# Input layernorm by batch, and a reordered opening, in a two-axis Mamba block with experts

## The reference, cut to what matters

```python
x = x + conv(ln(x, eps=1e-6))         # ln over the 64 channels, no weight
t = tokens(x)
t = t + experts(ln(t, eps=1e-5))      # 16 experts, the best 2 of each token
...
def dual_path(x, ...):                # conv above
    for i in range(6):
        xt = xt + mamba2(rmsnorm(xt, t_norm[i]), ...)   # sequences along time, per band
        xb = xb + mamba2(rmsnorm(xb, b_norm[i]), ...)   # sequences along bands, per time
def mamba2(x, ...):
    z, xBC, dt = split(x @ Win)
    x, B, C = split(silu(causal_conv4(xBC)))
    dt = softplus(dt + dt_bias)
    h[t] = exp(-dt * exp(A_log)) * h[t-1] + dt * x[t] * B[t];  y[t] = h[t] . C[t] + D * x[t]
    return rmsnorm(y * silu(z), gnorm) @ Wout
```

## Time and profile before

| | |
|---|---|
| three timed runs | 1254.06, 1256.41, 1258.2 us; median 1256.41 |
| the profiled execution | 1250.45 us, span 1248.5 us |
| TensorE | busy 1094.0 us, 88% of the span |
| VectorE | 836.2 us, 67% |
| ScalarE | 756.2 us, 61% |
| POOL | 312.1 us, 25% |
| mean granted TensorE clock | 0.966 of full speed |

### The profile page before, as it was taken

One profiled execution on the slowest core, in us unless ns is written; L12 is line 12 of the kernel. 1 busy time (PEld: TensorE's weight loads), 2 busy tenths in 40 slices (PEclk: granted clock), 3 DMA queues, 4 the chain that ended last, 5 costly groups with the idle time before them and its releaser, 6 DMA issues.

```text
span 1248.5 us, 46550 instructions
## 1 busy us (share of the span) xinstructions
PE 1094.0 (88%) x20216; PEld 568.9 (46%) x20216; DVE 836.2 (67%) x1219; ACT 756.2 (61%) x1450; POOL 312.1 (25%) x306
## 2 busy tenths in 40 slices
PE   2699989999999999989989999998987339999998
PEld 1355555555555545555454555555544223333332
DVE  4378666787666876668766687666876565656564
ACT  2477777677777677767777767776765113333332
POOL 7422232332223223232232322323222400000000
PEclk9799999999999999999999999999999558999999
DMA  4100110201111011110111101111000500000000
GB/s 84 23 18 7 30 30 19 44 5 31 31 31 33 2 31 31 31 32 4 30 31 31 33 2 31 31 31 33 9 7 14 85 1 1 1 9 9 1 9 9
DMA packets 66354, 28.75 MB, mean 23 GB/s; under 512 B 53416, under 2 KB 61928, under 8 KB 66152
## 3 DMA queue, kind: packets, MB, share of 16 engines
q1 hardware_dynamic: 66152, 25.78, 9.7%
HBM read 9.96 MB, written 1.05 MB: 9 GB/s over the span
## 4 chain that ended last, share of the span: by engine, by line
PE 72%; DVE 11%; issue 8%; ACT 6%; POOL 1%; DMA 1%; SPq 0%; ACTq 0%; DVEq 0%; POOLq 0%
PE ring L681 14%; PE ybank L766 10%; PE ring L893 6%; DVE em L1275 5%; PE ybank L908 5%; PE ring L746 5%; PE ring L899 4%; PE oss L778 4%; PE ring L705 4%; PE ring L691 4%; PE oss L781 3%; PE ring L633 2%; PE xtb L735 2%; PE ring L723 2%; ACT rstd L971 1%
## 5 line engine op out<-in xcount | busy, mean ns | idle before, releaser
L1275 DVE TENSOR_TENSOR em<-em,gs 128x1536 f32<-128x1536 f32 (+1 forms) x192 | 296.4, 1565 | 8.4 <-ACT em L1004 7.8
L1004 ACT ACTIVATE em<-ring 128x512 f32<-128x512 f32 x480 | 248.4, 597 | 9.5 <-PE ring L746 5.5
L766 PE MATMUL ybank<-em,xdt 64*32 64x64 f32 (+1 forms) x12288 | 186.7, 238 | 26.3 <-issue 19.5
L566 POOL TENSOR_TENSOR ysq<-yg 128x512 f32<-128x512 f32 x96 | 130.6, 1360 | 282.9 <-DVE yg L1295 282.9
L766 PEld LDWEIGHTS ybank<-em,xdt 64*32 64x32 f32 x12288 | 154.1, 106 | 83.9 <-issue 55.2
L746 PE MATMUL ring<-rt,lt 128*64 128x512 bf16 x960 | 144.9, 393 | 9.7 <-ACT em L1004 6.1
L1148 ACT ACTIVATE em<-ring 128x512 f32<-128x512 f32 x128 | 69.5, 595 | 137.4 <-PE ring L893 137.4
L1303 DVE TENSOR_TENSOR on<-oss,rr 128x256 f32<-128x256 f32 x96 | 40.6, 423 | 150.5 <-ACT rr L1014 150.5
L1446 DVE TENSOR_TENSOR em<-em,ring 128x512 f32<-128x512 f32 x128 | 82.2, 684 | 83.6 <-PE ring L899 81.3
L1012 ACT ACTIVATE rr<-oss,eps 128x256 f32<-128x256 f32 x96 | 45.5, 474 | 112.1 <-PE oss L781 111.9
L1282 DVE SCALAR_TENSOR_TENSOR yt<-xs,col,ybank 128x256 f32<-128x256 f32 x192 | 83.1, 473 | 35.5 <-PE ybank L766 35.3
(11 more groups left out here) (166 smaller groups left out, 1514.0 us busy)
## 6 DMA issues: line engine op xcount, KB each, us to landing
x_b<-x_t SPq DMA_DIRECT2D x48, 128.0 KB, 3.0
cm<-bc SPq DMA_DIRECT2D x24, 224.0 KB, 2.7
rt<-lt SPq DMA_DIRECT2D x120, 24.0 KB
cw<-in_L_conv_t_cw SPq DMA_DIRECT2D x6, 320.0 KB, 3.3
cw<-in_L_conv_b_cw SPq DMA_DIRECT2D x6, 320.0 KB, 3.1
x_in<-in_x SPq DMA_DIRECT2D x4, 256.0 KB, 4.4
xs<-in_L_ffn_w SPq DMA_DIRECT2D x2, 512.0 KB, 7.0
zs<-in_L_ffn_w SPq DMA_DIRECT2D x2, 512.0 KB, 9.1
```

The lines of the kernel that those rows point to most:

```text
L566: pool.tensor_tensor(out=ysq[c % 2][:], in0=yg[c % 2][:], in1=yg[c % 2][:], op=ALU.mult).then_inc(s_ysq, 1)
L766: mm = pe.matmul(ybank[QUAD * q:QUAD * (q + 1), ab, to:to + hi - lo], xdt[m % 2][rows, 8 * (i % 2) + 4 * first + q, r, :], em[rows, p % EM ...
L1004: emptied(act.activation(em[:, p % EM_SLOTS, :, HALF * j:HALF * (j + 1)], o.rearrange("p (h t) -> p h t", h=HEADS), ACT.Exp), "seg", n, i, ...
L1275: dve.tensor_tensor(e, e, gs[n % 2][:, i:i + 1, 0:wide].to_broadcast([P, HEADS, wide]), ALU.mult).then_inc(s_w, 1)
```

## The change

The first layernorm is made batch by batch: batch 0 first, batch 1 later, among VectorE's and ScalarE's other work of the opening. x of batch 1 is loaded behind the weights of pass 0, with a semaphore of its own. On TensorE B and C are projected ahead of x, the second batch's features and the parts are turned between the two projections of x, and mean(1, 0) comes behind z. C rows are sent before the wait for the template copies. On POOL the template's first nine selects, `tok1h` and the time parts come before the weights of pass 0; constants of the band pass and of the gate come behind `xdt`, with a fifth count `n_const[4]` that VectorE awaits in block 1. The second layernorm runs the same helpers half by half. The diff, cut:

```diff
     t.one("mean", 0, 1)
-    t.one("mean", 1, 0)
     t.two("dt", 0)
     t.one("dt_turned", 0)
+    t.two("bc", 0)
     t.one("cum", 0)
     t.two("x", 0, 0)
-    t.two("bc", 0)
+    t.one("parts", 0)
     t.two("x", 0, 1)
-    t.one("parts", 0)
     t.two("z", 0, 0)
     t.two("z", 0, 1)
+    t.one("mean", 1, 0)
     t.four("gram", 0)
...
# SP
+            x_load(0)
             weights_in(0)
+            x_load(1)
             weights_in(1)
             cross(0)
+            c_rows(0)
             sp.wait_ge(s_rep, 12)
-            c_rows(0)
             target_rows(0)
...
# POOL: h_b and tri[1] leave the front
-            const(pool.memset(h_b[:], 0.0))
...
+            parts_ones(0)
+            const(pool.memset(tok1h[:], 0.0))
+            select(tok1h[R_TOK:P].rearrange("p (a t) -> p a t", a=2), [[0, 2], [-1, HALF]], 0, 1, ALU.not_equal, 1.0)
+            n_const[1] = made[0]
+
+            const(pool.memset(rtmpl[:], 0.0))
+            for r in range(NPART):
+                select(rtmpl[0:R_TGT, LL], [[-1, HEADS], [0, HALF]], -HEADS * r, 1, ALU.not_equal, -1.0)
+                select(rtmpl[0:R_TGT, LH], [[-1, HEADS], [0, HALF]], -HEADS * r, 1, ALU.not_equal, -1.0)
+                select(rtmpl[R_HIGH:R_HIGH + R_TGT, HH], [[-1, HEADS], [0, HALF]], -HEADS * r, 1, ALU.not_equal, -1.0)
...
             weights_made(0)
+            pool.wait_ge(s_wp, 1)
             for blk in (LL, HH):
                 select(rtmpl[R_TOK:P, blk], [[0, HEADS], [1, HALF]], 0, -1, ALU.is_ge, FAR)
...
             for u in range(2):
                 const(pool.memset(xdt[u][:], 0.0))
+            n_const[3] = made[0]
+            const(pool.memset(h_b[:], 0.0))
+            const(pool.memset(tri[1][:], -1.0))
...
+            parts_ones(1)
...
             weights_made(1)
...
# PE
             mean(0, 1)
-            mean(1, 0)
             project_dt(0)
             turn_dt(0)
+            project_bc(0)
             sum_dt(0)
             project_x(0, 0)
-            project_bc(0)
+            pe.wait_ge(s_ln1, 2 * LN_STEPS)
+            to_features(s_tp, lambda j: sq[:, P * j:P * j + P], 1, 6)
+            turn_parts(0)
             project_x(0, 1)
-            pe.wait_ge(s_const, n_const[1])
-            turn_parts(0)
             project_z(0, 0)
             project_z(0, 1)
+            mean(1, 0)
             gram(0)
+            pe.wait_ge(s_x0, NCK)
             turn_x(0, 0)
...
# ACT
             rstd_of(0, 1)
-            square_x(1, 0)
+            norm_scalar(1, eps6)
+            copy_dt(0)
             exp_a(0)
-            exp_a(1)
-            rstd_of(1, 0)
-            copy_dt(0)
             softplus(0)
             act.preload_act_table_set("silu_and_others")
+            silu_bc(0)
             silu_x(0, 0)
-            silu_bc(0)
+            square_x(1, 0)
             silu_x(0, 1)
             silu_z(0, 0)
             silu_z(0, 1)
             act.preload_act_table_set("natural_log_exp_and_others")
+            rstd_of(1, 0)
+            exp_a(1)
             copy_gram(0)
...
# DVE (center: sum, scale, subtract; each over 1024 of the 2048 columns)
+            dve.wait_ge(s_ld[0], 16 * 2)
+            center(0)
+            sum_squares(0)
+            divide(0)
+            from_banks(0, 4, x_t)
...
             h_of(0, 1)
-            bias_dt(0)
-            finish_dt(0)
+            dve.wait_ge(s_ld[1], 16 * 2)
+            center(1)
             dve.wait_ge(s_const, n_const[1])
-            split_cum(0)
-            dve.wait_ge(s_const, n_const[2])
             for u in range(2):
                 dve.memset(lt[0:HALF, u], 0.0).then_inc(s_rep, 1)
...
+            sum_squares(1)
+            bias_dt(0)
+            divide(1)
+            finish_dt(0)
+            split_cum(0)
+            dve.wait_ge(s_const, n_const[2])
             for i in range(NPAIR):
                 dve.tensor_copy(rt[:, :, :, i, :].rearrange("p b h t -> p (b h) t"),
...
+            dve.wait_ge(s_rep, 4)
+            rows_of_cum(0)
+            from_banks(1, 6, x_t)
             dve.wait_ge(s_const, n_const[3])
             x_dt(0, 0)
...
# DVE, second layernorm
-            norm_vector(1)
-            from_banks(1, x2)
+            for k in (2, 3):
+                center(k)
+                sum_squares(k)
+                divide(k)
+            for k in (2, 3):
+                from_banks(k, 2 * (k % 2), x2)
```

More of the change, by code:

```diff
@@ L211, in build @@
         stat2 = sb("stat2", [P, NJ * 2])
-        s_ld = sem("x_loaded")
+        s_ld = [sem(f"x{b}_loaded") for b in range(NBATCH)]
         s_const = sem("constants_made")
@@ L358, in _, with x_load @@
         def _(sp):
-            for b in range(NBATCH):
+            def x_load(b):
                 for half in range(2):
-                    sp.dma_start(x_in[:, 8 * b:8 * (b + 1), half, :], token_rows(a["x"], b, half, 0, 8)).then_inc(s_ld, 16)
+                    sp.dma_start(x_in[:, 8 * b:8 * (b + 1), half, :], token_rows(a["x"], b, half, 0, 8)).then_inc(s_ld[b], 16)
             def weights_in(g):
@@ L496, in _, with parts_ones @@
             n_const[0] = made[0]
+            def parts_ones(s):
+                const(pool.memset(parts[s][:], 0.0))
+                for ab in range(2):
+                    rows = slice(HALF * ab, HALF * (ab + 1))
+                    const(pool.memset(parts[s][rows, :, R_TGT + NPART * ab:R_TGT + NPART * (ab + 1)], 1.0))
+            parts_ones(0)
[7 more added lines that the diff above has]
+                select(rtmpl[R_HIGH:R_HIGH + R_TGT, HH], [[-1, HEADS], [0, HALF]], -HEADS * r, 1, ALU.not_equal, -1.0)
             steps = [0]
@@ L554, in _ @@
                 const(pool.memset(xdt[u][:], 0.0))
+            n_const[3] = made[0]
+            const(pool.memset(h_b[:], 0.0))
+            const(pool.memset(tri[1][:], -1.0))
+            select(tri[1][:], [[1, P]], 0, -1, ALU.is_ge, 0.0)
+            select(tri[1][:].rearrange("p (a v) -> p a v", v=BANDS), [[-BANDS, P // BANDS], [0, BANDS]], 0, 1,
+                   ALU.is_ge, 0.0)
+            parts_ones(1)
+            for ab in range(2):
+                v = parts[1][HALF * ab:HALF * (ab + 1), :, R_SEQ:R_SEQ + 4]
+                const(pool.memset(v, 1.0))
+                select(v, [[0, NPAIR], [-BANDS, 4]], 0, 1, ALU.is_ge, 0.0)
+                select(v, [[0, NPAIR], [BANDS, 4]], BANDS - 1, -1, ALU.is_ge, 0.0)
             const(pool.memset(gate_w[:], 0.0))
@@ L1165, in norm_vector, with center @@
+            def center(k):
+                x, d, d2, st, st2 = norm_parts(k)
+                dve.tensor_reduce(st, x, AX.X, ALU.add).then_inc(s_ln1, 1)
                 dve.wait_ge(s_ln1, LN_STEPS * k + 1)
-                dve.tensor_scalar(stat[:], stat[:], 1.0 / C, None, ALU.mult).then_inc(s_ln1, 1)
+                dve.tensor_scalar(st, st, 1.0 / C, None, ALU.mult).then_inc(s_ln1, 1)
                 dve.wait_ge(s_ln1, LN_STEPS * k + 2)
-                dve.tensor_tensor(tm, xi, spread(stat[:], C), ALU.subtract).then_inc(s_ln1, 1)
+                dve.tensor_tensor(d, x, spread(st, C), ALU.subtract).then_inc(s_ln1, 1)
@@ L1169, in norm_vector, with sum_squares, divide @@
+            def sum_squares(k):
+                x, d, d2, st, st2 = norm_parts(k)
                 dve.wait_ge(s_ln1, LN_STEPS * k + 4)
-                dve.tensor_reduce(stat2[:], sq2, AX.X, ALU.add).then_inc(s_ln1, 1)
+                dve.tensor_reduce(st2, d2, AX.X, ALU.add).then_inc(s_ln1, 1)
+            def divide(k):
+                x, d, d2, st, st2 = norm_parts(k)
                 dve.wait_ge(s_ln1, LN_STEPS * k + 7)
-                dve.tensor_tensor(tm, tm, spread(stat2[:], C), ALU.mult).then_inc(s_ln1, 1)
@@ L1174, in from_banks @@
[L1174 to L1181, removed]
+                dve.tensor_tensor(d, d, spread(st2, C), ALU.mult).then_inc(s_ln1, 1)
+            def from_banks(k, into, dst):
+                for c in range(2):
+                    at = CK * (2 * (k % 2) + c)
+                    dve.wait_ge(s_tp, 2 * k + c + 1)
+                    dve.tensor_copy(dst[:, at:at + CK], bank[into + c][:]).then_inc(s_x0, 1)
```

79 lines of the change are left out of this document (30 added, 49 removed).

## The result

The changed kernel took 1249.77 us (median of 8 runs, 1244.37 to 1253.44), the kernel before beside it 1258.12 (8 runs, 1254.06 to 1261.97): ratio 0.9932, 95% interval 0.9909 to 0.9955, so 8.5 us less by the ratio (8.4 between the two medians). A second comparison gave 0.9929 (0.9902 to 0.9956). The forecast was 1247.3 in 1241.5 to 1252.5, 9.1 us less. The profiled execution of the changed kernel took 1247.55, its span is 1245.6.

The account below looks back on a forecast made before the run. It took the loop as bound by TensorE (busy 702 of 760 us) and the opening as a relay across engines. Opening minus 8.6 and second layernorm minus 0.5 from the median 1256.41 gave 1247.3 us, range 1241.5 to 1252.5.

Parts of the forecast that it names:

- Norm, h, weights: Opening, batch 0: features at 15.4 instead of 24.27, h at 20.8, weights ready by 22.6 and hidden.
- The wait put in: Opening, ScalarE: copying dt is held behind the second batch's Ln and Exp, starting at 28.0 instead of 32.00.
- B and C: Opening: projected by 33.5, C rows landed at about 37.5 instead of 56.56; most of that 19 us is slack.
- The ring: Opening: the gram's fourth bank waits for ScalarE's Ln until 49.15; first exponentials at 52.9 instead of 61.50, minus 8.6.
- Rival 1: Opening: target rows end last and x projections are fast; first exponentials at about 49.5, total 1243.9; chance 0.08.
- Rival 2: Opening: template copies wait on POOL's deferred constants, eight waits of 0.65; 4.4 lost, total 1251.7; chance 0.10.
- Rival 4: Opening: seven VectorE steps on the second batch's path each wait 1.65 beside POOL; 10.6 lost, total 1257.9; chance 0.03.
- Rival 3: Opening: TensorE stays at the lower clock from dt to the gram; 9.2 lost, total 1256.5; chance 0.05.
- The step that failed: Second layernorm: VectorE ends 0.7 to 2.0 later, eight fewer transposes give minus 1.8; taken as minus 0.5.
- The check on the loop: Loop: time from first exponentials to the second layernorm should be the same within 1 us, else the prediction is wrong.
- The range: Whole kernel: 1241.5 to 1252.5, from a gain of 5 to 13 with 1.5 for the base.

Follow-up runs that it names:

- Weights first: Changed kernel with POOL's weights of pass 0 again ahead of the nine template selects; first exponentials at 57.27 us (changed kernel: 51.99 and 54.30).
- dt first: Changed kernel with dt's chain ahead of the second batch's norm on ScalarE and VectorE; ratio to the kernel before 0.9954, first exponentials at 56.69 us.
- C rows late: Changed kernel with C rows again sent behind the wait for the template copies; first exponentials at 54.23 us (changed kernel: 51.99 and 54.30).
- B and C late: Changed kernel with B and C projected behind the first x and C rows sent behind the template copies; first exponentials at 56.24 us.

## Why the prediction was right, point by point, and where it was not

*Norm, h, weights.* x landed at 5.25 for 5.8, features at 15.03 for 15.4, h at 21.4 for 20.8, POOL's weights began at 17.56 for 16 to 18 and were ready at 20.8. Weights first shows that they were hidden: earlier weights moved nothing forward. *The wait put in* was right to 0.2: copy_dt at 27.82 for 28.0, behind the second batch's Exp; in other executions 29.2. The 0.2 is partly luck: h came 0.6 late, and the steps from h to the sum of squares took 6.0 for the forecast 6.65. dt first shows that the wait is real and that simply taking it away moves it to another place.

*B and C.* Their transfer is slack, as said: C rows late moved nothing. But the part that I did not price, the projection ahead of the sum of dt, is worth 2.0 in the changed kernel and most of 2.5 alone, as cover for TensorE's wait for dta and for its clock. The sum had it (3.9 for the first x, 3.70 measured); I had not named it as the gain.

*The ring.* The gram waited for ScalarE's Ln, and the first exponentials came at 51.99 for 52.9, in the four profiles at 53.7: minus 8.3 for minus 8.6. Rival 1 didn't occur. Rival 2 did in part: the copies lost 2.0 in three of the four profiles with this opening (5.88 in the one shown), over 0.6 each, which the prediction had named as a sign of being wrong. It was one copy held for a whole step of POOL, and not eight waits of 0.65; square_x(1, 0) then stood ahead of silu_x(0, 1) as described, at a price of 0.6 to 0.8 for the forecast 4.4. With the weights first the same path cost 3.6, from the second x's end at 43.68 to its silu at 47.31. The prediction had taken one fill of lt as evidence against it; that fill at 42.13 took 0.49 where it takes 0.42 alone, so it had been held a little, and beside other steps of POOL a fill takes 0.79 (dt first) and 0.91 (weights first). The rule of the Trainium skill that was weighed there (page "SBUF — State Buffer", section "Who interferes with whom") named this case rightly; the one copy's 1.89 beside POOL's step of 1.74 and the memset's 0.42 against 0.13 agree with it. Rival 4's price was never reached: the steps of h lost 0.7 together in one profile and 0.7 and 0.5 in the other. Rival 3 didn't occur; without B and C in the wait (B and C late) the first x alone was slow.

*The step that failed* is the second layernorm. VectorE's end came 0.4 later than before for the forecast 0.7 to 2.0, but "eight transposes instead of sixteen are left, minus 1.8" had the wrong end: behind sixteen transposes the clock comes up within the gate in five of six profiles, behind eight in none of seven, and the gate took 6.68 for 4.01. Minus 0.5 was plus 1.3. The total was near because this was small.

*The check on the loop* (the same within 1 us) failed too: plus 6.1 in the first pair, minus 12.9 between the second profile of before and of the changed kernel. It was a bad mark: the loop differs by 11.5 between two executions of the kernel before alone, and the sum against one profile's own time would have read 2.9 where the runs say 8.5.

*The range.* By its own terms (gain 5 to 13, 1.5 for the base) it runs from 1241.9 to 1252.9, 0.4 above what is written; nothing hangs on it.

What remains open: in the timed runs the gain is 8.5, the opening's 8.3 less the end's 1.3 to 1.7 and plus some 0.5 behind the gate is about 7.3; the difference is within the intervals. The norm by batch was never run alone. That dta comes 4 to 5 us earlier in the changed kernel (32.0 and 33.4 against 36.9 and 37.7) is read from the traces, but what this alone is worth, beside the 2.0 to 3.5 of B and C and the 3 of the constants, each read from one profile, is not shown. Why one block end is followed by a fall of the clock and another not was not tried.

## What to carry to other kernels

Where engines wait in fixed order, look for independent matmuls to put into the wait of the critical chain (here 2.0 and 2.5 us), and then at which bank, table or copy the released engine meets next: dt first moved dta four to five us forward and the first exponentials 2.4 to 4.7 back, and a few reorderings behind it turned it into the kernel with the lowest time. Don't split a burst of matmuls in front of a stage of small ones without asking what brought its clock up. Read a gain of this size stage by stage from marks in the traces of several executions; one profile's span can differ by 12 us for the same program.

## What the runs showed of the hardware that was not expected

- The loop of one unchanged program took 926.4 and 938.0 in two executions, with about 3 and 27 us at the lower clock. The Trainium skill, page "TensorE: Matmul & The Clock Gate", section "What's actually happening", says that the point at which the clock rises differs from run to run for the same kernel; the means in the opening, 3.41 and 3.75 in two executions of the changed kernel, would fit that, but the clock's row reads 1.00 beside both, so the trace doesn't show the point itself.
- A run of bfloat16 template copies on VectorE and POOL's steps hold each other: 0.42 against 0.13 for a memset of 32 columns, and one copy of the eight at 1.89 instead of 0.55 beside a POOL step of 1.74 (3.83 and 5.88 over the eight).
- 32 gate matmuls of 32 columns: 3.8 to 4.2 us behind sixteen transposes in five of six profiles, 6.9 with the granted clock at 0.50 throughout behind eight in seven of seven.
